# One transformer-like block on one core: the q, k, v projection issued as two 128x64 column tiles, with new call orders

## The reference, cut to what matters

```
agg_w, agg_b = per-batch 64x64 mixing weights and bias, from cond_128 by a small network and a softmax
m  = einsum('boi,bih->boh', agg_w, x) + agg_b          # mixing along the channels
q  = einsum('bsD,Ddh->bsdh', m, Wq) + bq               # 32 dims x 32 heads
k, v = the same with one head
p  = softmax(q[d, h] * k[e] / sqrt(32), over e)
o  = einsum('bsde,bse->bsd', p, v), summed over heads inside the first product
x  = x + o spread over the row
u  = grouped 1-d convolution of x (4 groups, 9 taps) + a context term + bias
out = x + u @ (scale * (unpack(packed_weight) - zero_point)).T + bias
```

## Time and profile before

| | |
|---|---|
| time of the runs, median of 3 | 423.92 us (418.14 to 425.28) |
| profiled execution, span from first to last instruction | 422.5 us |
| mean granted PE clock over the span | 0.996 of 2.4 GHz |
| PE busy | 408.1 us, 97% |
| POOL busy | 357.4 us, 85% |
| DVE busy | 356.2 us, 84% |
| PE weight loads busy | 346.0 us, 82% |
| ACT busy | 222.6 us, 53% |
| HBM traffic | 78.4 MB, 186 GB/s |

### The profile page before, as it was taken

How to read it: one execution, slowest core, us unless ns; L and a number is a source line. 1 busy time by engine, 2 the same in 40 slices (tenths; PEclk the granted TensorE clock), 3 DMA queues, 4 the chain that set the end, 5 groups by cost and what they waited for, 6 DMA issues and landing times.

```text
span 422.5 us, 6627 instructions
## 1 busy us (share of the span) xinstructions
PE 408.1 (97%) x2135; PEld 346.0 (82%) x2135; DVE 356.2 (84%) x594; ACT 222.6 (53%) x472; POOL 357.4 (85%) x358
## 2 busy tenths in 40 slices
PE   5979999999899999999999999999999999999997
PEld 4869988888788888888888888888888888888886
DVE  2679899999989999998979999989889899983422
ACT  4522896644637653774273565645463556572700
POOL 6034998999899999999998999999998889999920
PEclk9998999999999999999999999999999999999999
DMA  8984869067956036663069472919083452716112
GB/s 315 406 341 141 325 219 322 3 205 278 311 197 242 5 111 223 166 212 95 36 201 369 135 302 78 346 23 310 5 305 122 110 221 57 273 44 234 52 51 101
DMA packets 24954, 79.13 MB, mean 187 GB/s; under 512 B 6088, under 2 KB 6728, under 8 KB 22984
## 3 DMA queue, kind: packets, MB, share of 16 engines
q1 hardware_dynamic: 24760, 78.32, 52.9%
q10 hardware_dynamic: 144, 0.13, 0.1%
HBM read 61.14 MB, written 17.30 MB: 186 GB/s over the span
## 4 chain that ended last, share of the span: by engine, by line
PE 72%; DMA 2%; POOL 1%; DVE 1%; issue 1%; SPq 0%; DVEq 0%; POOLq 0%
PE p_f L1520 48%; PE p_conv L1514 18%; PE p_sm L1479 5%; DMA o_c<-o_dram 1%; PE p_sm L1499 1%; DMA o_dram<-o_sb 1%; PE p_conv L1520 0%; POOL c_lo L555 0%; DVE prob L1061 0%; POOL xc L545 0%; POOL xn L564 0%; DVE rden L1110 0%; POOL xc L548 0%; POOL xc L546 0%; DVE xn L1140 0%
## 5 line engine op out<-in xcount | busy, mean ns | idle before, releaser
L1520 PE MATMUL p_f<-w_ffn,u_hi 128*128 128x512 f32 (+1 forms) x512 | 194.7, 391 | 0.0
L1520 PE MATMUL p_f<-w_ffn,u_lo 128*128 128x512 f32 (+1 forms) x512 | 194.5, 389 | 0.0
L781 ACT ACTIVATE u_sb<-p_conv,u_bias,cols_sb 128x128 f32<-128x128 f32 x256 | 94.9, 461 | 37.9 <-PE p_conv L1514 37.5
L1520 PEld LDWEIGHTS p_f<-w_ffn,u_hi 128*128 128x128 f32 x512 | 96.2, 188 | 20.7 <-DVE u_lo L1130 0.3
L1520 PEld LDWEIGHTS p_f<-w_ffn,u_lo 128*128 128x128 f32 x512 | 96.1, 188 | 20.1
L555 POOL TENSOR_TENSOR c_lo<-xc,c_hi 128x516 fp32r<-128x516 f32 (+1 forms) x68 | 83.9, 1244 | 5.2 <-POOL xc L548 1.9
L771 ACT ACTIVATE c_hi<-xc 128x516 fp32r<-128x516 f32 (+1 forms) x68 | 41.4, 611 | 69.7 <-POOL xc L548 69.7
L564 POOL TENSOR_TENSOR xn<-xn,bias_n 128x1024 f32<-128x1024 f32 x32 | 76.4, 2404 | 0.2
L545 POOL TENSOR_TENSOR xc<-xc,o_c 128x384 f32<-128x384 f32 (+1 forms) x68 | 58.0, 853 | 7.9 <-DMA o_c<-o_dram 5.2
L1140 DVE TENSOR_TENSOR xn<-p_f,xn 128x512 f32<-128x512 f32 x64 | 43.2, 675 | 21.9 <-PE p_f L1520 21.5
L571 POOL TENSOR_TENSOR xn<-xn,o_sb 128x1024 f32<-128x1024 f32 x32 | 60.9, 1920 | 0.3
(11 more groups left out here) (127 smaller groups left out, 480.2 us busy)
## 6 DMA issues: line engine op xcount, KB each, us to landing
xn<-xn_in_in SPq DMA_DIRECT2D x16, 1024.0 KB, 6.9
out<-xn SPq DMA_DIRECT2D x31, 512.0 KB, 5.6
xc<-xc_in_in SPq DMA_DIRECT2D x15, 1032.0 KB, 8.7
xt<-xt_in_in SPq DMA_DIRECT2D x11, 1024.0 KB, 7.6
o_c<-o_dram SPq DMA_DIRECT2D x15, 256.0 KB
xn<-xt_in_in SPq DMA_DIRECT2D x3, 1024.0 KB, 15.2
xn<-wq_in SPq DMA_DIRECT2D x5, 512.0 KB, 8.4
xt<-xt_in_in SPq DMA_DIRECT2D x4, 512.0 KB, 9.7
```

The source lines that it names most:

```text
L781: ins = eng.activation(u_sb[:, g % 2, i * P:(i + 1) * P], p_conv[g % 2][:, i * P:(i + 1) * P], ACT.Identity, bias=u_bias[:, g, bat:bat + 1 ...
L1520: return mm(ffn_ps(k, part), u[:, (k // TU) % 2, r, t * P:(t + 1) * P], w_ffn[:, r, at:end], **flags)
```

## The change

Each f32 matmul of the projection and of the column sums is issued as two, one for the stationary operand's columns 0 to 63 and one for 64 to 127, writing PSUM partitions 0 to 63 and 64 to 127. `mix`, `conv` and `linear` stay as they were. `s_z`, `s_z_first` and `s_col` are raised once by each half, and the waits on them count to twice the number. All matmuls still have 128 rows of contraction and the same 96 moving columns; there are twice as many in these three functions, with half the weight columns each.

```diff
+COL_TILES = (slice(0, P // 2), slice(P // 2, P))
...
+        def projected(a):
+
+            return len(COL_TILES) * (a + 1)
+
...
-                    eng.wait_ge(s_z, (u - GUEST_END if u < GUEST_END + NXT else u - NXT) + 1)
+                    eng.wait_ge(s_z, projected(u - GUEST_END if u < GUEST_END + NXT else u - NXT))
...
+                eng.wait_ge(s_z_first, len(COL_TILES))
...
+                eng.wait_ge(s_col, len(COL_TILES))
...
-                    last = mm(z_ps(a)[:, t * W3:(t + 1) * W3], x_home(a)[:, t, r, :], w3[:, r, :], start=(r == 0), stop=(r == R - 1))
-                if t == TU - 1:
-                    last.then_inc(s_z, 1)
-                    if a not in Z_EARLY:
-                        copied = a + 1
+                    for q in COL_TILES:
+                        last = mm(z_ps(a)[q, t * W3:(t + 1) * W3], x_home(a)[:, t, r, q], w3[:, r, :], start=(r == 0), stop=(r == R - 1))
+                        if r == R - 1 and t == TU - 1:
+                            last.then_inc(s_z, 1)
+                if t == TU - 1 and a not in Z_EARLY:
+                    copied = a + 1
...
-                last = mm(col_ps, ones[:, :], w3[:, r, :], start=(r == 0), stop=(r == R - 1))
-                if r == R - 1:
-                    last.then_inc(s_col, 1)
+                for q in COL_TILES:
+                    last = mm(col_ps[q, :], ones[:, q], w3[:, r, :], start=(r == 0), stop=(r == R - 1))
+                    if r == R - 1:
+                        last.then_inc(s_col, 1)
...
-                last = mm(p_conv[0][:, 0:W3], xt[:, 0, 0, r, :], w3[:, r, :], start=(r == 0), stop=(r == R - 1))
-                if r == R - 1:
-                    last.then_inc(s_z_first, 1)
-                else:
+                for q in COL_TILES:
+                    last = mm(p_conv[0][q, 0:W3], xt[:, 0, 0, r, q], w3[:, r, :], start=(r == 0), stop=(r == R - 1))
+                    if r == R - 1:
+                        last.then_inc(s_z_first, 1)
+                if r < R - 1:
...
-                    last = mm(p_conv[1][:, 0:W3], xt[:, 0, 1, r, :], w3[:, r, :], start=(r == 0), stop=(r == R - 1))
-                last.then_inc(s_z, 1)
+                    for q in COL_TILES:
+                        last = mm(p_conv[1][q, 0:W3], xt[:, 0, 1, r, q], w3[:, r, :], start=(r == 0), stop=(r == R - 1))
+                        if r == R - 1:
+                            last.then_inc(s_z, 1)
```

The orders of the calls of all five engines are written anew, now out to the last unit. No call is added or dropped. PE's beginning:

```diff
             mlp(1)
+            context()
             mlp(2)
-            context()
+            keep_busy(6)
             turn_att()
-            keep_busy(6)
             mixing(0)
             mixing(1)
             mixing(2)
             mixing_bias()
             mixing(3)
-            read_flag()
             z_first(0)
             z_first(1)
             z_first(2)
@@ -1656,52 +2039,53 @@
             z_first(6)
             z_first(7)
             col_sum(7)
+            mix_first()
             z_second()
-            mix_first()
             mix(0)
             project(1, 0)
             project(1, 1)
+            project(2, 0)
             mix(1)
-            project(2, 0)
             project(2, 1)
             project(3, 0)
             project(3, 1)
-            mix(2)
             project(4, 0)
             project(4, 1)
             project(5, 0)
+            mix(2)
+            project(5, 1)
             conv(0, 0)
-            project(5, 1)
             conv(0, 1)
+            conv(0, 2)
+            read_flag()
             project(6, 0)
-            conv(0, 2)
             project(6, 1)
+            mix(3)
             conv(0, 3)
-            project(7, 0)
             conv(1, 0)
-            mix(3)
+            linear(0, 0)
+            linear(0, 1)
```

More of the change, by code:

```diff
@@ L679, in _ @@
             x_o(13)
[L681 to L693 removed]
+            add_o(8, 0)
+            add_o(8, 1)
@@ new lines, in _ @@
+            add_o(8, 2)
+            add_o(8, 3)
+            c_low(8, 0)
+            c_low(8, 1)
+            c_low(8, 2)
+            c_low(8, 3)
+            x_bias(14)
+            x_bias(15)
+            add_o(9, 0)
+            add_o(9, 1)
+            add_o(9, 2)
+            add_o(9, 3)
+            c_low(9, 0)
+            x_o(14)
+            x_o(15)
+            c_low(9, 1)
+            x_bias(16)
+            c_low(9, 2)
+            x_o(16)
+            c_low(9, 3)
+            x_bias(17)
@@ new lines, in _ @@
+            add_o(10, 0)
+            add_o(10, 1)
+            add_o(10, 2)
+            add_o(10, 3)
+            c_low(10, 0)
+            c_low(10, 1)
+            x_o(17)
+            c_low(10, 2)
+            c_low(10, 3)
+            x_bias(18)
+            x_o(18)
+            x_bias(19)
+            x_o(19)
+            add_o(11, 0)
+            add_o(11, 1)
+            add_o(11, 2)
+            add_o(11, 3)
+            c_low(11, 0)
+            c_low(11, 1)
+            c_low(11, 2)
@@ new lines, in _ @@
+            c_low(11, 3)
+            x_bias(20)
+            x_bias(21)
+            x_bias(22)
+            add_o(12, 0)
+            add_o(12, 1)
+            add_o(12, 2)
+            add_o(12, 3)
+            c_low(12, 0)
+            c_low(12, 1)
+            x_o(20)
+            x_o(21)
+            x_o(22)
+            c_low(12, 2)
+            c_low(12, 3)
+            x_bias(23)
+            x_o(23)
+            add_o(13, 0)
+            add_o(13, 1)
+            add_o(13, 2)
+            add_o(13, 3)
@@ new lines, in _ @@
+            c_low(13, 0)
+            c_low(13, 1)
+            c_low(13, 2)
+            c_low(13, 3)
+            x_bias(24)
+            x_bias(25)
+            x_o(24)
+            x_o(25)
+            add_o(14, 0)
+            add_o(14, 1)
+            add_o(14, 2)
+            add_o(14, 3)
+            c_low(14, 0)
+            c_low(14, 1)
+            c_low(14, 2)
+            c_low(14, 3)
+            x_bias(26)
+            x_bias(27)
+            add_o(15, 0)
+            add_o(15, 1)
@@ new lines, in _ @@
+            add_o(15, 2)
+            x_o(26)
+            add_o(15, 3)
+            c_low(15, 0)
+            c_low(15, 1)
+            c_low(15, 2)
+            x_o(27)
+            c_low(15, 3)
+            x_bias(28)
+            x_bias(29)
+            x_o(28)
+            add_o(16, 0)
+            add_o(16, 1)
+            add_o(16, 2)
+            add_o(16, 3)
+            c_low(16, 0)
+            c_low(16, 1)
+            c_low(16, 2)
+            c_low(16, 3)
+            x_o(29)
+            x_bias(30)
@@ L695, in _ @@
+            x_bias(31)
+            x_o(30)
+            x_o(31)
         @block.scalar
@@ new lines, in _ @@
+            conv(9, 3)
+            linear(15, 1)
+            mix(11)
+            linear(15, 2)
+            linear(15, 3)
+            linear(15, 4)
+            linear(15, 5)
+            linear(15, 6)
+            linear(15, 7)
+            linear(16, 0)
+            linear(16, 1)
+            conv(10, 0)
+            linear(16, 2)
+            conv(10, 1)
+            linear(16, 3)
+            linear(16, 4)
+            linear(16, 5)
+            linear(16, 6)
+            conv(10, 2)
+            linear(16, 7)
@@ new lines, in _ @@
+            conv(11, 1)
+            conv(11, 2)
+            linear(18, 6)
+            linear(18, 7)
+            linear(19, 0)
+            conv(11, 3)
+            linear(19, 1)
+            linear(19, 2)
+            linear(19, 3)
+            linear(19, 4)
+            linear(19, 5)
+            project(14, 0)
+            project(14, 1)
+            linear(19, 6)
+            linear(19, 7)
+            mix(13)
+            conv(12, 0)
+            linear(20, 0)
+            linear(20, 1)
@@ new lines, in _ @@
+            project(15, 1)
+            conv(13, 0)
+            mix(14)
+            conv(13, 1)
+            linear(22, 1)
+            linear(22, 2)
+            conv(13, 2)
+            linear(22, 3)
+            conv(13, 3)
+            mix(15)
+            linear(22, 4)
+            linear(22, 5)
+            linear(22, 6)
+            linear(22, 7)
+            linear(23, 0)
+            linear(23, 1)
+            linear(23, 2)
+            linear(23, 3)
+            linear(23, 4)
+            linear(23, 5)
```

1076 lines of the change are left out of this document (722 added, 354 removed).

## The result

The changed kernel takes 422.92 us, median of 4 runs (421.01 to 425.71), beside 421.03 us of the kernel before (4 runs, 416.49 to 425.28): 1.0132 of before, 95% interval 1.0068 to 1.0195. It is slower by 1.3%, 5.5 us, which is clear of zero and within 2%. The forecast was 416.8 us.

What follows compares the result with a forecast made beforehand. VectorE's attention was taken to bound the kernel until about 115 us, TensorE afterwards. Span 422.5 - 2.7 (start) - 3.3 (late) - 1.1 (units 6 to 9) = 415.4 us, plus 1.4 to the median: 416.8 us; range 410 to 425.

Steps and rivals of the forecast that it cites:

- its own signs of being wrong: Changed trace: a pair stepping by 0.107 us or more, first k_sb staying at 24 us, or TensorE waiting for c_lo after 120 us.
- The cost of a projection pass: TensorE projection: a column-tile pair steps in 0.088 us, two tiling changes cost 0.2 us, a unit takes 3.0 instead of 3.57.
- rival 2: Projection: column loads take turns, step stays 0.109 us; or dearer tiling changes, or c_lo bounds the end; 423.6 us; chance 0.23.
- rival 3: Projection: a load waits for its own tile's matmul, step 0.133 us, six units +5.8 us, 428 us; chance 0.03.
- rival 4: Projection: the two tiles stream one after the other, step 0.165 us, +20 us, 442 us; chance 0.06.
- The late credit of 3.3 us: TensorE after 115 us: six projection units each save 0.55 us, arriving in full as long as GpSimd keeps up.
- The credit of 1.1 us for units 6 to 9: Between 60 and 115 us, TensorE saves 2.2 us; half credited because VectorE leads there.
- The start, 2.7 us: Up to VectorE's first k_sb: later flag read, cheaper first passes and earlier first mix bring it 2.7 us earlier.
- costs up to 1.2 us if TensorE is sooner: VectorE at the start: head 0 summed behind the small network, last sum at 18.9 instead of 17.7 us; taken as hidden.
- The loads ahead of unit 1's x: Start of the queue: 1.5 MB, some 6 us, hidden since VectorE wants unit 1's projections some 10 us after their old start.
- The other moves: Reordered calls on GpSimd, ScalarE, VectorE and the load/store queue: no added instruction, no credit and no cost.
- all add_o of a piece now come before the c_low calls, so ScalarE's c_hi has time: GpSimd: this and an earlier last x_o bring the last c_lo about 1.9 us earlier; room, no credit.

Runs made afterwards that it cites:

- further execution of before: The unchanged kernel before, traced once more for comparison with the changed kernel's trace: span 415.8 us.
- e10_heads_and_loads: Changed kernel with loads and store moved off two queue round trips, head 0's sum ahead of the small network, first loads behind unit 2's x: 422.18 us, 1.0101.
- e6_old_first_loads: Changed kernel with packed weights, first conv input and bias loaded behind unit 2's x, as before: 423.95 us, 1.0137.
- e1_tiles_only: Kernel before with the column tiles alone, all five engines' call orders as before: 416.91 us, 0.9972.
- e7_tiles_queue: Kernel before with column tiles, and two loads of x (load_n 4 and 7) moved behind the attention output's spread: 415.25 us, 0.9929.
- e9: Changed kernel with loads and store moved off two queue round trips, and VectorE's sum over head 0 ahead of the small network: 421.69 us, 1.0077.
- e2: Changed kernel with one 128x128 tile instead of two column tiles, so only the orders are new: 427.81 us, 1.0237 of the kernel before.
- e5: Changed kernel with conv inputs of units 5 and 15 loaded before their saves and store(5) behind the spread: 420.97 us, 1.0082.
- e12: Changed kernel with loads and store moved off two queue round trips, but all five engines' orders as before up to about 75 us: 420.95 us, 1.0044.
- e14: Changed kernel with loads and store moved off two queue round trips, and GpSimd's add_o and c_low interleaved as before: 431.04 us, 1.0293.
- e15: Changed kernel, two queue round trips mended, add_o and c_low interleaved, first loads as before, mix(1) ahead of project(2, 0): 430.87 us, 1.0285.

## Why the prediction was wrong

The forecast credited 7.1 us and the change cost 5.5. Of the 12.6 us between them, 5.9 are credits that did not arrive (the tiles alone bring 1.2 us), and 6.7 are the new orders (1.0132 against 0.9972), which stood in the sum at nothing: that is the step that failed. The measured 422.92 us lies within the stated range of 410 to 425 us only because the range was laid round a base of 423.9 us; against the kernel run beside it the time moved the other way. Of its own signs of being wrong the forecast met one: TensorE waits for c_lo at 138, 166 and 393 us, and GpSimd's last c_lo ends at 396.5 us, where 5 us or more before 395.42 was forecast.

**The cost of a projection pass: right.** Unit 12's projection in the changed kernel's TensorE timeline, which answers to the earlier trace rows:

```profile
227.73 0.39 PE L1900 MATMUL p_f<-w_ffn,u_lo 128*128 128x512 f32 x1
228.05 2.86 PE L1859 MATMUL p_sm<-w,xt 128*64 128x96 f32 x64
230.84 0.50 PE L1900 MATMUL p_f<-w_ffn,u_hi 128*128 128x512 f32 x1
231.18 0.40 PE L1900 MATMUL p_f<-w_ffn,u_lo 128*128 128x512 f32 x1
```

From 227.73 to 231.18 us are 3.45 us; less two product steps of 0.227 a unit costs 3.0 us, as forecast, and 0.58 us less than the 4.03 us that the same distance takes in the further execution of before. The first tile's passes give the pair by itself, first at the higher level (changed kernel), then at the lower (e10_heads_and_loads):

```profile
15.45 0.36 PE L1944 MATMUL p_sm<-w,ones 128*64 128x96 f32 x4
15.62 0.36 PE L1955 MATMUL p_conv<-w,xt 128*64 128x96 f32 x4
15.78 0.36 PE L1944 MATMUL p_sm<-w,ones 128*64 128x96 f32 x4
```

```profile
17.21 0.53 PE L1955 MATMUL p_conv<-w,xt 128*64 128x96 f32 x4
17.53 0.53 PE L1944 MATMUL p_sm<-w,ones 128*64 128x96 f32 x4
```

Two pairs take 0.165 and 0.32 us: 0.083 and 0.160 us a pair, against a forecast range of 0.082 to 0.093 and 0.160. The granted clock does not show the lower level in e10 there, but in e6_old_first_loads it is 0.50 from 15.2 to 18.4 us, with the same steps of 0.32 us. The entry into the tiles costs 0.32 less 0.227, the exit 0.34 less 0.227 us, 0.1 each as taken. Rivals 2, 3 and 4, as prices of a pass, are out; the last condition of rival 2, GpSimd's c_lo as the bound, came in part (below). The Trainium skill's rule (TensorE: Matmul & The Clock Gate, Part 3) that a load overlaps a matmul only in another row group would have given 0.133 us by the working of rival 3; both tiles here lie in the same row groups, and the measurement decides against it for these shapes.

**The late credit of 3.3 us: too large.** It held that from 115 us "every microsecond of TensorE work counts, as long as GpSimd keeps up". GpSimd did not quite. In e1_tiles_only four whole units after 115 us save 0.58 us each, and three half units, each by itself between products, only 0.12 (2.13 us against 2.25 from the product before to the second one behind), since each half pays both changes of tiling: 2.7 us. But the lead over the further execution of before grows only from 0.2 us at tile 4 to 1.2 us at tile 31. The rest, 1.6 us, goes between tiles 12 and 13, where TensorE waits for c_lo:

```profile
203.41 0.47 PE L1520 MATMUL p_conv<-c_hi,cw_hi 128*128 128x512 f32 x1 [0.99 <-POOL c_lo L560]
```

The forecast saw GpSimd's small room and put it into half a sentence of rival 2 instead of taking it off the credit. e7_tiles_queue, with the queue mended ahead of this place, loses 0.4 us there.

**The credit of 1.1 us for units 6 to 9: nothing arrived.** In e1_tiles_only the lead is 0.8 us at tile 0 and 0.2 us at tile 4; its waits for c_lo between them, at 65 and 109 us, are 1.15 us longer than before's.

**The start, 2.7 us: wrong.** The 1.4 us from slow passes and the base of 24.63 us for k_sb came from one execution in which TensorE's level was low until 22 us. The further execution was expected to show, if that start was chance, a first k_sb near 21 to 22 us and a span near 416 us. It did: its k_sb starts at 20.89 us, the changed kernel's at 21.02. First the further execution of before, then the changed kernel:

```profile
10.70 7.16 DVE L997 TENSOR_REDUCE w<-xn 128x32 f32<-128x1024 f32 x7
...
20.89 0.19 DVE L1041 TENSOR_TENSOR k_sb<-p_sm,qkv_bias 128x32 f32<-128x32 f32 x1 [1.47 <-PE p_sm L1489]
```

```profile
9.16 0.16 DVE L1216 SCALAR_TENSOR_TENSOR att<-p_sm,cols_sb 64x8 f32<-64x8 f32 x1 [9.16 <-PE p_sm L1986]
...
12.68 6.89 DVE L1229 TENSOR_REDUCE w<-xn 128x32 f32<-128x1024 f32 x7
...
21.02 0.19 DVE L1273 TENSOR_TENSOR k_sb<-p_sm,qkv_bias 128x32 f32<-128x32 f32 x1 [0.23 <-PE p_sm L1869]
```

VectorE now stands idle for the small network, whose last matmul is behind context() on TensorE, and its last sum ends at 19.6 instead of 17.9 us. TensorE, sooner with its passes, waits for the sums (0.17, 0.57 and 0.64 us). The forecast named this ("costs up to 1.2 us if TensorE is sooner") and counted 0. Undoing VectorE's half of it (e9) gained nothing, though its last sum still ends only at 19.0 us; so no run shows what this costs.

**The loads ahead of unit 1's x: the cover failed.** TensorE waits for x, and mix(1), now behind project(2, 0), comes at 31.99 instead of 25.79 us. First the changed kernel, then the further execution of before:

```profile
24.30 2.86 PE L1859 MATMUL p_f<-w,xt 128*64 128x96 f32 x64 [1.00 <-DMA xt<-xt_in_in]
29.41 2.65 PE L1859 MATMUL p_conv<-w,xt 128*64 128x96 f32 x32 [2.25 <-DMA xt<-xt_in_in]
31.99 1.17 PE L1879 MATMUL p_sm<-z_own,mix_t 128*128 128x96 f32 x4
```

```profile
25.79 0.69 PE L1499 MATMUL p_sm<-z_own,mix_t 128*128 128x96 f32 x4 [0.42 <-ACT z_own L751]
```

VectorE waits 2.53 us for that mix and takes up unit 1's k at 33.8 us, against 31.0 in the further execution of before. The cover counted unit 1's x alone, and that held: its projection is only 2.7 us later (24.30 against 21.63 us), where VectorE wanted it 9.4 us behind its old start. What it left out is that mix(1) now stands behind unit 2's x, and about 1.1 us of the 6.2 are the stretch at the lower clock. Yet e6, which removes this stop, did not gain; it has a stop of 2.78 us for unit 3's x in its place. That the stop costs time is not shown, only that it is there.

**The other moves "add no instruction", with no credit and no cost: the step that failed.** The new orders cost 9.9 us with one tile (e2) and 6.7 us with two (the changed kernel against e1). An order was priced by what it adds, not by what it makes late. The half sentence "stores that step past a save wait behind it" looked at the store; the round trip that waits behind the store was the path. That stop is shown (e5): 4 us by the traces, 2 by the ratios, which are not clear of the noise. That "all add_o of a piece now come before the c_low calls, so ScalarE's c_hi has time" was counted as room for GpSimd; it puts the first c_lo of a piece behind two more add_o, 4 us, and in e12 TensorE pays 2.54 us for it at once.

**The account.** In points of the time of before: tiles -0.3; new start about +0.5; new orders behind it about +0.6; the queue's stop +0.5. The sum is +1.3, as measured, because each share is the distance between two of these runs; no single share is known better than to 0.3 to 0.7 points. Open is which calls within the two halves cost: single moves undone in the start gave nothing, with stops of their own (e6, e9, e10), and the one tried in both halves made it worse (e14, e15).

## What to carry to other kernels

Where a fixed order is rewritten along with the work, measure the two apart first; here a right price for the work (3.0 us a unit) said nothing of the total. A saving on the busiest engine counts only up to the slack of the engine that feeds it, so let that slack cap the credit in the same sum. In a queue, look for round trips (save, then spread) and for what stands between the two; taking it out cured one of two places here, and at the other, with the load ahead of the save, the save took longer instead. Before a sum is built on the start of one trace, read a second execution of the same kernel: here they differ by 3.7 us at the first k_sb.

## What the hardware showed that was not expected

Two column tiles over the same 128 rows load and stream at the same time: a pair of 128x64 tiles with 96 f32 moving columns steps once in 0.083 us at 2.4 GHz and in 0.160 us at 1.2 GHz. A half unit between products gains almost nothing from them (0.12 us), a whole one 0.58.

A wait of 2.71 us at 163.5 to 166.2 us was followed by a granted clock of 0.57 over the next 4 us, and so cost TensorE 1.6 us beyond itself. It does not always come so: a wait of 2.25 us that ends near 29.3 us was followed by 3.4 us at 0.50 in the changed kernel's trace and by none in e5's, and one of 3.22 us at 37.8 us in e1_tiles_only by none.

A round trip whose second half was issued behind a store and a load took 8.6 us from its issue (148.04 us) to the end of GpSimd's wait (156.6 us); without the two between, at most 5.8 us (e5).

A subtraction of VectorE over 512 elements a row took 0.68 us with GpSimd idle, and 2.85 us where GpSimd's split of the convolution weights (2.69 us) ran at the same time (e10). The trace has the same, 2.81 us at 26.77 us. VectorE's product and sum beside that split in the further execution of before (26.95 to 29.3 us) kept to their 0.68 us, so it depends on the instruction.
